# Where the last q/k piece, the first norms and a quarter of the values stand around the attention projection

## Chip, core, metric

The kernel runs on one core of one Trainium2 chip. The metric is device time in microseconds of one execution, the median of several.

## What is computed

One adaLN transformer block on x of shape 2 x 2048 x 256, float32: LayerNorm with modulation, causal attention with random features (16 heads of width 16, 128 features), projection and gated residual, a second LayerNorm, and a feed-forward part with a top-2 router over 4 experts that share Wi and Wo and differ by a rank-4 term.

```python
h = layernorm(x) * (1 + ca) + sa
q, k, v = split(h @ W_attn + b_attn)                  # q, k scaled by 1/sqrt(16)
phi(z) = exp(z @ omega - 0.5 * sum(z * z)) / sqrt(m)  # per head
y = (phi_q . cumsum(phi_k v)) / (phi_q . cumsum(phi_k) + 1e-6)
x = x + ga * (y @ W_proj + b_proj)
h = layernorm(x) * (1 + cb) + sb
w = top2(softmax(h @ Wg.T + bg))
x = x + gb * sum_e w_e * (relu(h @ Wi.T + (h @ A_e.T) @ B_e.T) @ Wo.T)
```

The term sum(z * z) is what the kernel calls norms.

## The kernel before

The 4096 tokens are worked in NB = 8 blocks of T = 512, each four tiles of 128. Every engine runs its own hand-written program; semaphores tie them together, and nothing else decides the order. A loop runs blocks 0 to 6 with `front_next` true, so that block n + 1's front part (LayerNorm 1, q and k, norms, values, the first features) is woven into block n. Block 7 is written out behind the loop without a front part.

q and k come in four pieces j = 0 to 3 of 128 rows by 512 tokens (`qk`, L416). A piece is two halves over the contraction (`ks` [0] and [1]), three matmuls each: products are made from a rounded part and a rest (`split3`, L377: L380 to L382). Piece j lies in PSUM bank `qk_bank[j]`: pa[0], pa[1], ring[2], ring[3]. ScalarE then makes the rounded copy and the square of a piece (`front_qk`, L779: L782, L783) and counts `sq_ready`, and VectorE makes the rest (`split_qk`, L1031) and counts `qk_split`. `norms` (L426) multiplies the squares of two pieces by a matrix that sums over a head; it waits until both are squared. Half 0 (pieces 0 and 1) goes to `norm_bank[0]`, half 1 (pieces 2 and 3) to ring[0]. ScalarE rounds them (L789), VectorE makes their rest (L1040) and counts `norm_split`. `values` (L436) makes the values of the four token tiles into the products banks pb[0] and pb[1], 6 matmuls a tile; VectorE moves them to v_ones (L1046).

The stretch around the change is `after_attend`. On TensorE: the first half of piece 3, norms 0, the transposes of y (`y_transpose`, L606; ScalarE copies them out, L843), the second half of piece 3, the projection into pa (`projection`, L620), norms 1, all values, then `ffn_head`: eight transposes of the normalised tokens (L638) into ring[3] and ring[1], the small matmuls of the router logits and low-rank terms (L643), and the first base matmuls, which read h_r and h_l. VectorE adds the projection to the residual (L1155), takes statistics (L1158, L996 to L999), GpSimd makes the reciprocal deviation (L1333, L1336), VectorE normalises tiles 0 and 1 (L1004) and ScalarE tiles 2 and 3 (L848). After the transposes ScalarE makes h_f (L852) and its rounded copy h_r (L856), VectorE the other half of h_f (L1021) and h_l (L1028). h_r and h_l held block n + 1's first LayerNorm output until then, which q, k and values read.

SyncE (`front_moves`, L329) stores each piece of q and k and each half of the norms to DRAM as they are split, and gathers them as xq, from which the features of block n + 1 are made (L493, L498), the first of them among the experts' matmuls of block n.

Of the kernel before, what the change touches and what calls it, by code (L numbers as in the profile page):

```python
# [43 lines left out]
NT = T // P  # L44
# [54 lines left out]
def wait(eng, signal, n, c):  # L99
    eng.wait_ge(signal.sem, signal.at(n, c))  # L100


def build(nc, x, w_attn, b_attn, w_proj, b_proj, omega, wg, bg, wi, wo, lora_a, lora_b, cond, wmod,
          consts, norm_rows, out, parts_out, norms_out):
    ctx = ExitStack()
    with ctx:
# [102 lines left out]
        prod = ctx.enter_context(nc.psum_tensor("prod", [P, NT, 2, P], F32))  # L209
        pb = [prod[:, 2 * b:2 * b + 2].rearrange("p c k m -> p (c k m)") for b in range(2)]  # L210
        qk_bank = [pa[0], pa[1], ring[2], ring[3]]
        norm_bank = [pa[0], ring[0]]
        z_bank = [ring[3], ring[1], ring[0], ring[2]]
        score_bank = lambda q, a: (pa if q else pb)[a]
        proj_bank = lambda tile: pb[tile % 2] if tile < 2 * TILES else ring[tile % 4]
# [160 lines left out]
        def _(pe):  # L376
# [49 lines left out]
            def norms(n, half):  # L426

                wait(pe, sq_ready, n, 2 * half + 2)
                if half == 0:
                    wait(pe, qk_split, n, 1)  # L430
                for j in (2 * half, 2 * half + 1):
                    mm = pe.matmul(norm_bank[half][j * VA:(j + 1) * VA, :], headsum, qk_sq[:, j, :],
                                   start=True, stop=True)
                mm.then_inc(norm_mm.sem, 1)

            def values(n):  # L436
                for t in range(NT):
                    dst = pb[t // 2][:, t % 2 * C:(t % 2 + 1) * C]
                    tt = slice(t * P, (t + 1) * P)
                    for k in range(KT):  # L440
                        mm = split3(dst, h_r[:, k, tt], h_l[:, k, tt],
                                    wa_r[:, k, 2 * C:3 * C], wa_l[:, k, 2 * C:3 * C], k == 0, k == KT - 1)
                    if t % 2:
                        mm.then_inc(v_ps.sem, 1)
# [164 lines left out]
            def projection(n, front_next):  # L609
                wait(pe, yT_done, n, KT)  # L610
                if front_next:
                    wait(pe, qk_split, n + 1, 2)
                    wait(pe, norm_split, n + 1, 1)
                row = n // BLOCKS_PER_ROW
                for t in range(NT):
                    dst = pa[t // 2][:, t % 2 * C:(t % 2 + 1) * C]
                    for k in range(KT):
                        w = wp_ga[:, row, k, :] if isinstance(n, int) else \
                            wp_ga[:, bass.ds(row, 1), k, :].rearrange("p o c -> p (o c)")
                        mm = pe.matmul(dst, yT[:, k, t * P:(t + 1) * P], w, start=k == 0, stop=k == KT - 1)  # L620
                    if t % 2:
                        mm.then_inc(prj_ps.sem, 1)
# [9 lines left out]

            def ffn_head(n, front_next):

                for t in range(NT):
                    wait(pe, h2n_ready[t // 2], n, t % 2 + 1)
                    for k, dst in enumerate((ring[3], ring[1])):
                        mm = pe.transpose(dst[:, t * P:(t + 1) * P], tok[:, t, k * P:(k + 1) * P], ident)  # L638
                        if t == NT - 1:
                            mm.then_inc(h2_ps.sem, 1)  # L640
                for k in range(KT):
                    wait(pe, h2_full[k], n, 1)
                    mm = pe.matmul(ring[2][:], low_t[:, k, :], h_f[:, k, :], start=k == 0, stop=k == KT - 1)  # L643
                    if k == 0:
                        mm.then_inc(tok_free.sem, 1)
                mm.then_inc(lg_ps.sem, 1)
                base(n, 0, [0])
                wait(pe, lg_done, n, 1)
                base(n, 0, [1])
                rows = slice(LOGIT_ROW, LOGIT_ROW + E)  # L650
                for t in range(NT):
                    mm = pe.transpose(pa[0][:, t * E:(t + 1) * E], lg[rows, t * P:(t + 1) * P], ident[rows, rows])
                mm.then_inc(lt_ps.sem, 1)
                base(n, 1)
                if front_next:
                    wait(pe, norm_split, n + 1, 2)
                base(n, 2)
                wait(pe, low_high, n, 1)
                base(n, 3)
# [81 lines left out]
            def after_attend(n, front_next):  # L741
                if front_next:
                    qk(n + 1, 3, [0])
                    norms(n + 1, 0)
                y_transpose(n)
                if front_next:
                    qk(n + 1, 3, [1])
                projection(n, front_next)
                if front_next:
                    norms(n + 1, 1)  # L750
                    values(n + 1)
                ffn_head(n, front_next)
                masks(n)
                experts(n, front_next)
# [9 lines left out]
        def _(act):  # L764
# [80 lines left out]
            def ffn(n, front_next):  # L845
                wait(act, ln2_pool, n, 2)
                for t in range(2, NT):
                    act.activation(tok[:, t, :], xr[:, t, :], ACT.Identity, bias=shift[:, t:t + 1],  # L848
                                   scale=rstd[:, t:t + 1]).then_inc(h2n_ready[1].sem, 1)
                wait(act, mod2c_set, n, 1)  # L850
                wait(act, h2_ps, n, 1)
                act.activation(h_f[:, 0, :], ring[3][:], ACT.Identity, bias=mod2_cols[:, KT:KT + 1],  # L852
                               scale=mod2_cols[:, 0:1]).then_inc(h2_full[0].sem, 1)
                for k in range(KT):
                    wait(act, h2_full[k], n, 1)
                    act.activation(h_r[:, k, :], h_f[:, k, :], ACT.Copy).then_inc(h2_r.sem, 1)  # L856
                wait(act, lg_ps, n, 1)
                act.activation(lg, ring[2][:], ACT.Copy).then_inc(lg_done.sem, 1)
                act.activation(low.bitcast(F32R), ring[2][0:LROWS, :], ACT.Copy).then_inc(low_high.sem, 1)
                wait(act, rt, n, 10)  # L860
                act.activation(exo[:], ex[:], ACT.Exp).then_inc(rt_exp.sem, 1)
                tile = 0
                for f in range(FT + 3):
                    if f < FT:
                        wait(act, z1_ps, n, f + 1)
                        if f >= 4:
                            wait(act, g_low, n, f - 3)
                        act.activation(g[:, f % 4, :], z_bank[f % 4][:], ACT.Relu).then_inc(r1_done.sem, 1)  # L868
                    if f == 0:
                        wait(act, rho_ps, n, 1)  # L870
                        act.activation(rho, pa[1][:], ACT.Copy).then_inc(rho_done.sem, 1)
                    for _ in range(AHEAD.get(f, 0) if front_next else 0):
                        features(n + 1, tile // TILES, [tile % TILES])
                        tile += 1
                    if 1 <= f <= FT:
                        k = f - 1
                        wait(act, g_sum, n, k + 1)
                        if k == 0 and front_next:
                            for signal in qk_out:
                                wait(act, signal, n + 1, signal.per)  # L880
                        if k >= 3:
                            wait(act, wo_mm, n, k - 2)
                        act.activation(g_r[:, k % 3, :], g[:, k % 4, :], ACT.Copy).then_inc(g_high.sem, 1)  # L883
# [12 lines left out]
            def after_attend(n, front_next):  # L896
                if front_next:
                    front_qk(n + 1, 0)
                    front_qk(n + 1, 1)
                    front_norm(n + 1, 0)  # L900
                y_copy(n)
                if front_next:
                    front_qk(n + 1, 2)
                    front_qk(n + 1, 3)
                    front_norm(n + 1, 1)
                ffn(n, front_next)
# [9 lines left out]
        def _(dve):  # L916
# [364 lines left out]

            def after_attend(n, front_next):
                if front_next:
                    split_norm(n + 1, 0)
                    split_qk(n + 1, 2)
                residual(n)
                if front_next:
                    split_qk(n + 1, 3)
                normalize_apply(n, xr, ln2_pool, h2n_ready[0])
                if front_next:  # L1290
                    split_norm(n + 1, 1)
                h2_copy(n)
                if front_next:
                    values(n + 1, [0])
                split_h(n, h2_r, 1, h2_parts)
                if front_next:
                    values(n + 1, [1])
                ffn_rest(n, front_next)
# [111 lines left out]
```

## Time and profile before

| | us |
|---|---|
| median of 3 runs | 826.2 (823.42, 826.2, 828.61) |
| the profiled execution | 827.64 |
| its span, first to last instruction | 825.9 |
| TensorE busy | 766.3 |
| VectorE busy | 547.2 |
| ScalarE busy | 409.9 |
| mean granted TensorE clock, of full | 0.980 |

Rows of a timeline give start, duration, engine, line, what was written from what, and the idle time of the engine before it with what ended it. Ends of matmuls are modelled and overlap the next one's start, so intervals are best read from start to start. A matmul row in plain float32 counts two instructions per matmul of the program.

### The profile page before, as it was taken

The page shows a single profiled execution, that of the slowest core. Times are in us where ns is not written, and L with a number is a line of the kernel's source. Part 1 is how long each engine was busy: PE and PEld are TensorE (multiplying, and loading weights), DVE is VectorE, ACT ScalarE, POOL GpSimd, SP SyncE. Part 2 cuts the span into 40 slices and gives each one's busy share as a digit, 9 for nine tenths or more (in the row PEclk, how much of TensorE's full clock was granted, in tenths as well). Part 3 has the DMA queues.
Part 4 walks back from the last instruction along what each step waited for, and adds up shares of the span by engine and source line. Part 5 has one row for each costly group of instructions (what it writes and reads, how often), then busy time and mean ns, then how long its engine had stood idle before and what let it go on. Part 6 is the DMA issues. An engine that isn't in the chain of part 4 may idle for free.

```text
span 825.9 us, 16957 instructions
## 1 busy us (share of the span) xinstructions
PE 766.3 (93%) x6138; PEld 605.5 (73%) x6138; DVE 547.2 (66%) x1289; ACT 409.9 (50%) x758; POOL 46.9 (6%) x62
## 2 busy tenths in 40 slices
PE   2989999999999999999999999999999999998696
PEld 2767767977688767977688766977679776886466
DVE  5546666776766766776766766776667767666356
ACT  2365544664366444654466545555446643663222
POOL 1101000010000100010000100010000100010000
PEclk9969999999999999999999999999999999999689
DMA  8680073202802064101722046020732028010000
GB/s 270 145 203 5 2 207 81 77 0 70 213 2 76 0 172 113 51 26 51 191 43 76 0 117 169 0 76 0 206 79 76 0 74 209 2 52 2 0 1 26
DMA packets 46540, 65.37 MB, mean 79 GB/s; under 512 B 8716, under 2 KB 22840, under 8 KB 46392
## 3 DMA queue, kind: packets, MB, share of 16 engines
q1 hardware_dynamic: 46520, 65.10, 29.4%
q8 instruction: 13, 0.21, 0.1%
q14 instruction: 7, 0.06, 0.0%
HBM read 39.87 MB, written 25.17 MB: 79 GB/s over the span
## 4 chain that ended last, share of the span: by engine, by line
PE 85%; DVE 9%; ACT 2%; issue 1%; SPq 1%; DMA 1%; DVEq 0%; POOL 0%; POOLq 0%; ACTq 0%
PE pa L514 11%; PE prod L529 7%; PE ring L493 6%; PE ring L380 6%; PE pa L380 5%; PE ring L381 4%; PE ring L382 4%; PE pa L382 4%; PE pa L381 4%; PE prod L548 4%; PE pa L620 4%; PE ring L498 3%; PE ring L643 2%; PE prod L514 2%; PE ring L696 2%; PE prod L538 2%
## 5 line engine op out<-in xcount | busy, mean ns | idle before, releaser
L514 PE MATMUL pa<-phq,phkT 128*128 128x128 f32 x896 | 115.6, 276 | 0.0
L514 PEld LDWEIGHTS pa<-phq,phkT 128*128 128x128 f32 x896 | 108.4, 192 | 2.4 <-issue 1.6
L821 ACT ACTIVATE phq<-ring 128x512 f32<-128x512 f32 x96 | 58.9, 614 | 91.3 <-PE ring L493 90.3
L1078 DVE TENSOR_TENSOR am_phk<-pa,const 128x512 f32<-128x512 f32 x112 | 74.3, 686 | 33.2 <-PE pa L514 33.2
L1231 DVE SCALAR_TENSOR_TENSOR am_phk<-ring,am_phk 128x512 f32<-128x512 f32 x64 | 44.3, 692 | 53.2 <-PE ring L696 53.2
L380 PE MATMUL pa<-wo_r,qk_r 128*128 128x256 f32 x256 | 72.1, 282 | 0.6 <-DVE qk_l L1236 0.6
L382 PE MATMUL pa<-wo_l,qk_r 128*128 128x256 f32 x256 | 72.2, 282 | 0.0
L883 ACT ACTIVATE qk_r<-phq 128x512 fp32r<-128x512 f32 x64 | 40.5, 632 | 63.7 <-DVE phq L1240 63.7
L381 PE MATMUL pa<-wo_r,qk_l 128*128 128x256 f32 x256 | 71.8, 281 | 0.0
L529 PE MATMUL prod<-am_phk,v_ones 128*32 128x256 f32 x1024 | 61.9, 382 | 4.6 <-DVE tg L1109 4.6
L380 PE MATMUL ring<-h_r,wi_r 128*128 128x512 f32 x128 | 57.9, 452 | 4.2 <-DVE am_phk L1231 3.6
L821 ACT ACTIVATE phkT<-ring 128x512 f32<-128x512 f32 x96 | 59.3, 618 | 0.0
L493 PE MATMUL ring<-xq,omega_x 100*128 100x512 f32 x192 | 58.9, 428 | 0.0
L821 ACT ACTIVATE am_phk<-ring 128x512 f32<-128x512 f32 x96 | 52.9, 614 | 11.3 <-PE ring L498 11.3
L868 ACT ACTIVATE phq<-ring 128x512 f32<-128x512 f32 x64 | 37.6, 587 | 32.8 <-PE ring L684 32.8
L529 PEld LDWEIGHTS prod<-am_phk,v_ones 128*32 128x32 f32 x1024 | 31.3, 109 | 28.9 <-DVE am_phk L1078 6.3
L381 PE MATMUL ring<-h_r,wi_l 128*128 128x512 f32 x128 | 50.9, 398 | 0.0
L382 PE MATMUL ring<-h_l,wi_r 128*128 128x512 f32 x128 | 50.8, 397 | 0.0
L380 PEld LDWEIGHTS pa<-wo_r,qk_r 128*128 128x128 f32 x256 | 48.4, 189 | 2.6 <-DVE qk_l L1236 1.0
L381 PEld LDWEIGHTS pa<-wo_r,qk_l 128*128 128x128 f32 x256 | 48.4, 189 | 1.4
L382 PEld LDWEIGHTS pa<-wo_l,qk_r 128*128 128x128 f32 x256 | 48.1, 188 | 0.0
L1236 DVE TENSOR_TENSOR qk_l<-phq,qk_r 128x512 fp32r<-128x512 f32 x64 | 43.8, 685 | 5.9 <-ACT qk_r L883 5.6
(189 smaller groups left out, 1568.2 us busy)
## 6 DMA issues: line engine op xcount, KB each, us to landing
xq<-qk_parts SPq DMA_DIRECT2D x48, 512.0 KB
qk_parts<-qk_r SPq DMA_DIRECT2D x32, 256.0 KB, 3.6
qk_parts<-qk_l SPq DMA_DIRECT2D x32, 256.0 KB, 4.0
tok<-in_L_attn_x SPq DMA_DIRECT2D x8, 512.0 KB, 4.9
xr<-in_L_attn_x SPq DMA_DIRECT2D x8, 512.0 KB, 4.0
out_x<-tg SPq DMA_DIRECT2D x16, 256.0 KB, 2.2
norm_parts<-norm_r SPq DMA_DIRECT2D x16, 128.0 KB, 3.6
norm_parts<-norm_l SPq DMA_DIRECT2D x16, 128.0 KB, 5.1
```

The costliest lines, as they stand in the source:

```text
L380: pe.matmul(dst, w_r, v_r, start=first, stop=False, skip_group_check=shared)
L381: pe.matmul(dst, w_l, v_r, start=False, stop=False, skip_group_check=shared)
L382: return pe.matmul(dst, w_r, v_l, start=False, stop=last, skip_group_check=shared)
L493: mm = pe.matmul(dst[:], omega_x[:, k // 2 * M:(k // 2 + 1) * M], xq[:, p // HALF, k % 2, p % HALF, :], start=True, stop=True)
L514: mm = pe.matmul(score_bank(q, a)[:, tt], phkT[:, q % 2, a, tt], phq[:, q // 2 % 2, 2 * (q % 2) + a, tt], start=True, stop=True)
L529: mm = pe.matmul(prod[j * VA:(j + 1) * VA, c], v_ones[:, c, GROUP * gr + j, :], both, start=True, stop=True)
L821: act.activation(dst, src, ACT.Exp).then_inc(exp_done.sem, 1)
L868: act.activation(g[:, f % 4, :], z_bank[f % 4][:], ACT.Relu).then_inc(r1_done.sem, 1)
L883: act.activation(g_r[:, k % 3, :], g[:, k % 4, :], ACT.Copy).then_inc(g_high.sem, 1)
L1078: dve.tensor_tensor(am[:, 2 * (q % 2) + a, :].rearrange("p (c t) -> p c t", c=NT), score_bank(q, a)[:].rearrange("p (c t) -> p c t", c=NT) ...
L1231: dve.scalar_tensor_tensor(r2[:, f % 2, :], z_bank[f % 4][:], 0.0, rho, ALU.max, ALU.mult).then_inc(r2_done.sem, 1)
L1236: dve.tensor_tensor(g_l[:, k % 3, :], g[:, k % 4, :], g_r[:, k % 3, :].bitcast(F32), ALU.subtract).then_inc(g_low.sem, 1)
```

## The change

Within `after_attend`, for blocks 0 to 6:

- TensorE: the transposes of y come before norms 0, and the second half of piece 3 comes behind the projection, directly ahead of norms 1. Only three token tiles of the values follow; the fourth is made in `ffn_head` behind the eight token transposes.
- Norms 0 go to pb[0], a products bank, instead of pa[0]. So the projection waits no longer for `norm_split` 1, and `values` does (in the setup too, for block 0). `norms` waits no longer for `qk_split`. `ffn_head` waits for `qk_split` 4 and `norm_split` 1.
- ScalarE does piece 2 ahead of the copy of y and norms 0 behind it, and waits for the last values (`v_ps`) before it writes h_r. VectorE splits piece 2 ahead of norms 0.

```diff
--- before.py
+++ after.py
@@ -209,7 +209,7 @@
         prod = ctx.enter_context(nc.psum_tensor("prod", [P, NT, 2, P], F32))
         pb = [prod[:, 2 * b:2 * b + 2].rearrange("p c k m -> p (c k m)") for b in range(2)]
         qk_bank = [pa[0], pa[1], ring[2], ring[3]]
-        norm_bank = [pa[0], ring[0]]
+        norm_bank = [pb[0], ring[0]]
         z_bank = [ring[3], ring[1], ring[0], ring[2]]
         score_bank = lambda q, a: (pa if q else pb)[a]
         proj_bank = lambda tile: pb[tile % 2] if tile < 2 * TILES else ring[tile % 4]
@@ -426,15 +426,14 @@
             def norms(n, half):
 
                 wait(pe, sq_ready, n, 2 * half + 2)
-                if half == 0:
-                    wait(pe, qk_split, n, 1)
                 for j in (2 * half, 2 * half + 1):
                     mm = pe.matmul(norm_bank[half][j * VA:(j + 1) * VA, :], headsum, qk_sq[:, j, :],
                                    start=True, stop=True)
                 mm.then_inc(norm_mm.sem, 1)
 
-            def values(n):
-                for t in range(NT):
+            def values(n, tiles=range(NT)):
+                wait(pe, norm_split, n, 1)
+                for t in tiles:
                     dst = pb[t // 2][:, t % 2 * C:(t % 2 + 1) * C]
                     tt = slice(t * P, (t + 1) * P)
                     for k in range(KT):
@@ -610,7 +609,6 @@
                 wait(pe, yT_done, n, KT)
                 if front_next:
                     wait(pe, qk_split, n + 1, 2)
-                    wait(pe, norm_split, n + 1, 1)
                 row = n // BLOCKS_PER_ROW
                 for t in range(NT):
                     dst = pa[t // 2][:, t % 2 * C:(t % 2 + 1) * C]
@@ -632,12 +630,17 @@
 
             def ffn_head(n, front_next):
 
+                if front_next:
+                    wait(pe, qk_split, n + 1, 4)
+                    wait(pe, norm_split, n + 1, 1)
                 for t in range(NT):
                     wait(pe, h2n_ready[t // 2], n, t % 2 + 1)
                     for k, dst in enumerate((ring[3], ring[1])):
                         mm = pe.transpose(dst[:, t * P:(t + 1) * P], tok[:, t, k * P:(k + 1) * P], ident)
                         if t == NT - 1:
                             mm.then_inc(h2_ps.sem, 1)
+                if front_next:
+                    values(n + 1, [NT - 1])
                 for k in range(KT):
                     wait(pe, h2_full[k], n, 1)
                     mm = pe.matmul(ring[2][:], low_t[:, k, :], h_f[:, k, :], start=k == 0, stop=k == KT - 1)
@@ -741,14 +744,14 @@
             def after_attend(n, front_next):
                 if front_next:
                     qk(n + 1, 3, [0])
+                y_transpose(n)
+                if front_next:
                     norms(n + 1, 0)
-                y_transpose(n)
+                projection(n, front_next)
                 if front_next:
                     qk(n + 1, 3, [1])
-                projection(n, front_next)
-                if front_next:
                     norms(n + 1, 1)
-                    values(n + 1)
+                    values(n + 1, range(NT - 1))
                 ffn_head(n, front_next)
                 masks(n)
                 experts(n, front_next)
@@ -851,6 +854,8 @@
                 wait(act, h2_ps, n, 1)
                 act.activation(h_f[:, 0, :], ring[3][:], ACT.Identity, bias=mod2_cols[:, KT:KT + 1],
                                scale=mod2_cols[:, 0:1]).then_inc(h2_full[0].sem, 1)
+                if front_next:
+                    wait(act, v_ps, n + 1, 2)
                 for k in range(KT):
                     wait(act, h2_full[k], n, 1)
                     act.activation(h_r[:, k, :], h_f[:, k, :], ACT.Copy).then_inc(h2_r.sem, 1)
@@ -897,10 +902,10 @@
                 if front_next:
                     front_qk(n + 1, 0)
                     front_qk(n + 1, 1)
+                    front_qk(n + 1, 2)
+                y_copy(n)
+                if front_next:
                     front_norm(n + 1, 0)
-                y_copy(n)
-                if front_next:
-                    front_qk(n + 1, 2)
                     front_qk(n + 1, 3)
                     front_norm(n + 1, 1)
                 ffn(n, front_next)
@@ -1281,8 +1286,8 @@
 
             def after_attend(n, front_next):
                 if front_next:
+                    split_qk(n + 1, 2)
                     split_norm(n + 1, 0)
-                    split_qk(n + 1, 2)
                 residual(n)
                 if front_next:
                     split_qk(n + 1, 3)
```

The next pieces show what each engine's program has in a row. Line numbers in those of the changed kernel are its own. First TensorE around the transposes of y, before: ring0 and ring1 take the transposes, ring3 is piece 3's bank, and L432 is `norms`.

```order
L432 MATMUL pa0<-phq,const 32x512 [waits qk_split]
L432 MATMUL pa0<-phq,const 32x512
L100 REGISTER_ALU
L606 MATMUL ring0<-const,tg 128x128 [waits y_step]
L606 MATMUL ring0<-const,tg 128x128 x3
L606 MATMUL ring1<-const,tg 128x128 x4
L380 MATMUL ring3<-h_r,wa_r 128x512
L381 MATMUL ring3<-h_r,wa_l 128x512
L382 MATMUL ring3<-h_l,wa_r 128x512
L620 ISA [waits norm_split,qk_split,yT_done]
L620 MATMUL pa0<-wp_ga,phkT 128x256
```

The same place in the changed kernel, where L605 is the transpose (L100 only prepares a wait), L430 `norms` and L618 the projection:

```order
L605 MATMUL ring0<-const,tg 128x128 [waits y_step]
L605 MATMUL ring0<-const,tg 128x128 x3
L605 MATMUL ring1<-const,tg 128x128 x4
L100 REGISTER_ALU
L430 MATMUL prod<-phq,const 32x512 [waits sq_ready]
L430 MATMUL prod<-phq,const 32x512
L618 ISA [waits qk_split,yT_done]
L618 MATMUL pa0<-wp_ga,phkT 128x256
```

The norms went behind the transposes, and the half piece into ring3 left the place between transposes and projection. Where it went is this piece of the changed TensorE program, behind the projection:

```order
L618 MATMUL pa1<-wp_ga,phkT 128x256 x4
L380 MATMUL ring3<-h_r,wa_r 128x512
L381 MATMUL ring3<-h_r,wa_l 128x512
L382 MATMUL ring3<-h_l,wa_r 128x512
L430 MATMUL ring0<-phq,const 32x512 [waits sq_ready]
L430 MATMUL ring0<-phq,const 32x512
L380 MATMUL prod<-wa_r,h_r 128x256 [waits norm_split]
```

Before, the projection was followed by the norms into ring0 at once; now the last half piece stands between them. ScalarE in the same stretch, before (ring2 and ring3 are pieces 2 and 3):

```order
L789 ACTIVATE norm_r<-pa0 64x512 [waits norm_mm]
L100 ISA
L843 ACTIVATE phkT<-ring0 128x512 [waits yT_ps]
L100 REGISTER_ALU
L843 ACTIVATE phkT<-ring1 128x512 [waits yT_ps]
L100 REGISTER_ALU
L782 ACTIVATE qk_r<-ring2,qk_bias 128x512 [waits qk_ps]
L783 ACTIVATE phq<-ring2,qk_bias 128x512
L100 REGISTER_ALU
L782 ACTIVATE qk_r<-ring3,qk_bias 128x512 [waits qk_ps]
L783 ACTIVATE phq<-ring3,qk_bias 128x512
```

and in the changed kernel:

```order
L785 ACTIVATE qk_r<-ring2,qk_bias 128x512 [waits qk_ps]
L786 ACTIVATE phq<-ring2,qk_bias 128x512
L100 ISA
L846 ACTIVATE phkT<-ring0 128x512 [waits yT_ps]
L100 REGISTER_ALU
L846 ACTIVATE phkT<-ring1 128x512 [waits yT_ps]
L792 ACTIVATE norm_r<-prod 64x512 [waits norm_mm]
L100 REGISTER_ALU
L785 ACTIVATE qk_r<-ring3,qk_bias 128x512 [waits qk_ps]
L786 ACTIVATE phq<-ring3,qk_bias 128x512
```

Piece 2 moved ahead of the copies of y, and the norms behind them.

## Rows read from the trace of the kernel before

**Rows 1.** The page, part 1: busy time and share of the span.

```profile
PE 766.3 (93%) x6138; PEld 605.5 (73%) x6138; DVE 547.2 (66%) x1289; ACT 409.9 (50%) x758; POOL 46.9 (6%) x62
```

**Rows 2.** The chain that ended last: start us, us, what.

```profile
393.62 3.72 PE pa L620 x16
```

**Rows 3.** TensorE's timeline, 476 to 500: start us, us, engine, line, operation.

```profile
476.38 1.93 PE L529 MATMUL prod<-am_phk,v_ones 128*32 128x256 f32 x32 [0.48 <-DVE tg L1109]
...
485.55 1.05 PE L432 MATMUL pa<-phq,const 128*32 128x512 f32 x4
486.54 1.09 PE L606 MATMUL ring<-const,tg 128*128 128x128 f32 x8
487.38 0.48 PE L380 MATMUL ring<-h_r,wa_r 128*128 128x512 f32 x1
...
487.93 0.40 PE L382 MATMUL ring<-h_l,wa_r 128*128 128x512 f32 x1
488.50 3.71 PE L620 MATMUL pa<-wp_ga,phkT 128*128 x16 [0.18 <-ACT phkT L843]
492.15 1.05 PE L432 MATMUL ring<-phq,const 128*32 128x512 f32 x4
493.13 0.39 PE L380 MATMUL prod<-wa_r,h_r 128*128 128x256 f32 x1
...
495.96 0.27 PE L382 MATMUL prod<-wa_l,h_r 128*128 128x256 f32 x1
496.22 1.39 PE L638 MATMUL ring<-const,tok 128*128 128x128 f32 x8
498.43 1.98 PE L643 MATMUL ring<-am_phk,low_t 128*128 128x512 f32 x4 [0.82 <-ACT am_phk L852]
499.85 0.79 PE L380 MATMUL ring<-h_r,wi_r 128*128 128x512 f32 x1
```

**Rows 4.** ScalarE's timeline in the same stretch.

```profile
481.08 0.69 ACT L782 ACTIVATE qk_r<-pa,qk_bias 128x512 fp32r<-128x512 f32 x1 [2.31 <-PE pa L382]
481.67 0.68 ACT L783 ACTIVATE phq<-pa,qk_bias 128x512 f32<-128x512 f32 x1
...
487.23 1.09 ACT L843 ACTIVATE phkT<-ring 128x512 f32<-128x512 f32 x2
...
496.03 1.09 ACT L848 ACTIVATE tok<-xr,shift,rstd 128x256 f32<-128x256 f32 x2 [2.18 <-POOL shift L1336]
497.60 0.78 ACT L852 ACTIVATE am_phk<-ring,mod_cols 128x512 f32<-128x512 f32 x1 [0.48 <-PE ring L638]
```

**Rows 5.** VectorE's timeline in the same stretch.

```profile
475.72 0.42 DVE L1109 TENSOR_TENSOR tg<-prod,rden 128x256 f32<-128x256 f32 x1
...
485.46 0.42 DVE L1109 TENSOR_TENSOR tg<-prod,rden 128x256 f32<-128x256 f32 x1
...
495.75 0.73 DVE L1004 TENSOR_SCALAR tok<-xr,mv,rstd 128x256 f32<-128x256 f32 x2 [0.41 <-POOL rstd L1333]
```

**Rows 6.** Timeline of the setup, TensorE and VectorE.

```profile
30.41 0.39 PE L380 MATMUL prod<-wa_r,h_r 128*128 128x256 f32 x1
...
30.08 0.67 DVE L1040 TENSOR_TENSOR norm_l<-pa,norm_r 64x512 fp32r<-64x512 f32 x1
```

**Rows 7.** Timelines of SyncE's queue and of TensorE's first features.

```profile
490.92 2.38 SPq L353 DMA_DIRECT2D xq<-norm_parts  x4
...
508.88 0.47 PE L493 MATMUL prod<-xq,omega_x 100*128 100x512 f32 x1
```

**Rows 8.** Stretches: PE, PEld, DVE, ACT, POOL busy, then PEclk, DMA, GB/s.

```profile
200.00:760.00 560.00, 541.20 (x4440) 429.85 (x4438) 386.34 (x911) 295.58 (x549) 31.25 (x34) 1.00 0.29 79
764.00:766.00 2.00, 1.60 (x32) 0.88 (x32) 0.87 (x4) 0.00 (x0) 0.00 (x0) 0.75 0.00 0
774.00:776.00 2.00, 2.00 (x8) 1.64 (x7) 0.74 (x2) 0.00 (x0) 0.00 (x0) 0.69 0.00 0
```

**Rows 9.** TensorE's timeline in the last block.

```profile
760.02 1.93 PE L529 MATMUL prod<-am_phk,v_ones 128*32 128x256 f32 x32 [1.18 <-DVE tg L1109]
```

More of the change, by code:

```diff
@@ L743, in after_attend @@
                     qk(n + 1, 3, [0])
-                    norms(n + 1, 0)
                 y_transpose(n)
                 if front_next:
-                    qk(n + 1, 3, [1])
+                    norms(n + 1, 0)
                 projection(n, front_next)
                 if front_next:
+                    qk(n + 1, 3, [1])
                     norms(n + 1, 1)
-                    values(n + 1)
+                    values(n + 1, range(NT - 1))
                 ffn_head(n, front_next)
@@ L899, in after_attend @@
                     front_qk(n + 1, 1)
-                    front_norm(n + 1, 0)
+                    front_qk(n + 1, 2)
                 y_copy(n)
                 if front_next:
-                    front_qk(n + 1, 2)
+                    front_norm(n + 1, 0)
                     front_qk(n + 1, 3)
```

## Prediction

> **What bounds the kernel now.** I read the page's engine table first. TensorE is busy for 93% of the span [rows 1], so what counts is the work in its queue and the gaps in it. The chain of waits gives the rhythm: the projection of one block starts at 393.62, that of the next at 488.50 [rows 2, 3], a period of 94.9 us, and seven of the eight blocks run with the next block's front part woven in. The change touches only the few microseconds around the projection of these seven, and a little of the setup. TensorE's timeline for that stretch [rows 3] shows the order to be followed, those of ScalarE and VectorE [rows 4, 5] what each step waits for. Three gaps are visible. The projection starts after an idle time of 0.18 us. The eight transposes L638 take 1.39 us where those of L606 take 1.09, so they lose 0.30. Before L643 TensorE is idle for 0.82 us. Together 1.3 us per block: that is all the change can win here, 9.1 us over seven blocks.
>
> The two later gaps end a chain that starts with the projection: the residual and its statistics, GpSimd's deviation, tok from VectorE at 495.75 and from ScalarE until 496.03 + 1.09 = 497.12, the last transposes, h_f on ScalarE from 497.60 to 498.38, L643 at 498.43 [rows 3 to 5]. TensorE fills it with the second norms (492.15 to 493.13) and all 24 matmuls of the values.
>
> **The change, step by step,** on the clock of the block in rows 3. I go from start to start, since modelled ends overlap.
>
> *The transposes of y come before the first norms.* They need VectorE's last division, which ends at 485.46 + 0.42 = 485.88. In the same wait one group earlier the division ended at 476.14 and TensorE began at 476.38 [rows 3, 5], so the wake costs 0.24 and the transposes start at 486.12. Before, the norms (L432, 0.99 us) lay there and hid it; now the queue, free at 485.55, stalls for 0.57. This wait is new. From the transposes' start to the next start are 0.84 (486.54 to 487.38), so the norms start at 486.96 and, 0.98 later, the queue reaches the projection at 487.94. Its other condition is ScalarE's copy of y: the transposes end at 487.21, the second copy takes some 0.6 behind that, and the wake was 0.18 (487.23 + 1.09 = 488.32, start at 488.50), so 488.03. ScalarE has done piece 2 before that, since its bank is full before 485.55. The projection starts at 488.03 instead of 488.50: 0.47 won. The first norms cost nothing more in a products bank: the same instructions, and VectorE has read that bank for its last division, on which the transposes ahead of them wait.
>
> *The last half piece follows the projection.* From projection to next start are 3.65, so it starts at 491.68, and its last matmul ends 0.95 later (487.38 to 487.93 + 0.40), at 492.63. The second norms now stand right behind it, and they multiply the squares of this very piece (they wait for sq_ready to reach 4). ScalarE must pass over the bank twice for that: in rows 4 the pair runs from 481.08 to 482.35, 1.27 us, and I let it start 0.04 after the matmul. So the squares are there at 493.94, and with a wake of 0.1 the norms start at 494.05. In the old order the same pair ran beside the projection. The queue alone would have been ready at about 492.5, so this is a new stall of 1.5 us, and everything on TensorE is queued behind it: norms, values, the transposes of the tokens. I see nothing that hides it.
>
> *Three quarters of the values, the transposes, then the last quarter.* Norms to values 0.98 gives 495.03. 18 of 24 matmuls at 0.12 each (493.13 to 495.96 for 23 steps) are 2.1 us: 497.15. The normalised tokens are there by then, since their chain starts 0.47 earlier with the projection: ScalarE's at about 496.65. VectorE's split of the last piece needs the squares at 493.94, and VectorE comes to it only after the statistics, about then, so it delays nothing. The transposes run without a gap from 497.25 to 498.34, and the last quarter of the values (0.7 us) covers ScalarE's h_f, 0.78 plus a wake of 0.05: L643 at 499.15. So the old gap of 0.82 is hidden, all but 0.1 to 0.2. ScalarE's new wait for the last values before it overwrites h_r puts its copy at about 499.2, with h_l on VectorE behind it. Base's first matmul is due 1.42 after L643 (498.43 to 499.85), at 500.57, and h_l comes at about 499.2 + 0.6 + 0.65 + a wake = 500.6. I price this at 0, at most 0.2.
>
> *Sum.* L643 starts at 499.15 instead of 498.43: 0.72 later in each of seven blocks, 5.0 us. What follows (router, masks, experts, the next attention) hangs on L643, so nothing gives it back. Bounds: the wakes seen run from 0.04 to 0.24 and four of them are in the sum, h_l may cost 0.2, and the stall behind the last piece cannot be far under ScalarE's 1.27. That gives 0.3 to 1.1 per block, 2.1 to 7.7.
>
> *Setup.* values(0) now waits for VectorE's first norm split, which ends at 30.08 + 0.67 = 30.75, where it started at 30.41 [rows 6]; with a wake 0.4 us, once. Bounds 0.3 and 0.6.
>
> *Transfers.* The first norm split comes behind ScalarE's copy of y, at about 489.5, some 1.5 us later, and SP's norm stores and the gathers behind them move with it. SP issued the last four of these gathers from 490.92 to 493.30, and their data are first wanted by the features at 508.88, 15 us later [rows 7]. Slack enough: 0.
>
> So the profiled execution, 827.64 us with a span of 825.9, would become 827.6 + 5.0 + 0.4 = 833.0. The median of the three runs shown is 826.2, 1.4 below it; on that scale I forecast 831.6. That is 0.7% slower, and counts as the same: 1%, 8.3 us, is about what a measurement of this kernel can tell from no change.
>
> **The rivals.** *A, slower: TensorE's clock falls.* The change puts stalls of 0.6 and 1.5 us into 8 us, and behind the longer one stand norms on 32 of 128 columns. Over the loop the granted clock is 1.00, which is 2.4 GHz. In the last block, which has no front work in its waits (1.18 us before L529 [rows 9], and shorter ones after it), it fell to 1.2 GHz in the slice 764 to 766 and came back in the slice 774 to 776, ten microseconds later [rows 8]. By these rows a fall costs half of up to 10 us of work; I take 3.5 to 5. In three of seven blocks that is 10.5 or more, 842; in all seven 25 to 35, 857 and up. It outweighs everything else from two blocks on. Against it: the wait of 0.82 between transposes has not done it in any block, and dense matmuls stand on both sides. The Trainium skill, "TensorE: Matmul & The Clock Gate", section "A second HAM failure mode: psum-queue depth-cycling", names frequent short idles between groups of matmuls as a way to lose the clock. By that rule the time would be this rival's; the last block agrees with it, the loop does not show it.
>
> *B, faster: the stall behind the last piece is hidden, and the gaps won count.* If the norms started at once, L643 would be 0.47 earlier with the projection and some 0.7 earlier for the two gaps covered, 1.2 us in all: 826.2 - 8.4 + 0.4 = 818. For it speaks only that the old trace does not show the wait; against it, that ScalarE cannot square a bank before it is written.
>
> *C: it comes out even.* The wakes are all at the low end and the stall before the transposes of y is half of what I take: 0.1 to 0.2 per block, 827 to 828.
>
> **How the numbers follow.** Forecast 0.60 (its own range 828.5 to 834.5), A 0.22, B 0.05, C 0.13. The line of slower by over 1% is 834.5: 0.03 of the forecast lies above it, and 0.19 of A (with one fall it stays below), which makes 0.22. Faster needs 818 or less: 0.03, out of B. The rest, 0.75, is the same. The range runs from 826, under C, to 841, just short of A in three blocks, and leaves out most of A.
>
> **What would show it.** In the changed profile: TensorE's wait of the second norms for ScalarE's square, idle 1.3 or more, seven times; a wait of the transposes of y for VectorE's tg of 0.3 to 0.6; the wait for h_f down from 0.82 to under 0.3; the token transposes in 1.1 us; a period of 95.6; a granted clock of 1.00 between 200 and 760. Wrong would be a period at or under 94.9, a clock below 1.00 in the loop, or a wait for gathers before the features.

## The result, and the profile after

The changed kernel took 830.23 us (median of 13 runs, 828.86 to 831.49) against 826.26 (13 runs): ratio 1.0056, 95% interval 1.0044 to 1.0068. It is slower by half a percent, inside the range, and under the 831.6 forecast. The prediction took 1%, 8.3 us, as about what a measurement can tell from no change; this interval, 0.24% wide, tells much less than that. The profiled execution took 830.51 us with a span of 828.7; before, 827.64 with 825.9.

TensorE is less busy in a longer span, on page part 1 [rows 1]:

```profile
PE 762.5 (92%) x6138; PEld 606.8 (73%) x6138; DVE 546.6 (66%) x1289; ACT 411.2 (50%) x758; POOL 47.1 (6%) x62
```

The chain of waits has the projections of two blocks 95.25 us apart, where they were 94.88 by rows 2 and 3. This distance is called the period below:

```profile
394.22 3.65 PE pa L618 x16
...
489.47 3.65 PE pa L618 x16
```

TensorE's timeline of the same block as in rows 3. L605 is the transposes of y, L430 the norms, L618 the projection, L639 the token transposes, L646 what was L643:

```profile
486.14 0.48 PE L380 MATMUL ring<-h_r,wa_r 128*128 128x512 f32 x1
...
486.69 0.40 PE L382 MATMUL ring<-h_l,wa_r 128*128 128x512 f32 x1
487.40 1.09 PE L605 MATMUL ring<-const,tg 128*128 128x128 f32 x8 [0.30 <-DVE tg L1114]
488.42 1.05 PE L430 MATMUL prod<-phq,const 128*32 128x512 f32 x4
489.40 3.72 PE L618 MATMUL pa<-wp_ga,phkT 128*128 x16
492.77 0.58 PE L380 MATMUL ring<-h_r,wa_r 128*128 128x512 f32 x1
...
493.42 0.40 PE L382 MATMUL ring<-h_l,wa_r 128*128 128x512 f32 x1
495.17 1.05 PE L430 MATMUL ring<-phq,const 128*32 128x512 f32 x4 [1.36 <-ACT phq L786]
496.15 0.39 PE L380 MATMUL prod<-wa_r,h_r 128*128 128x256 f32 x1
...
498.38 1.04 PE L639 MATMUL ring<-const,tok 128*128 128x128 f32 x8
499.18 0.36 PE L380 MATMUL prod<-wa_r,h_r 128*128 128x256 f32 x1
...
500.24 1.98 PE L646 MATMUL ring<-am_phk,low_t 128*128 128x512 f32 x4
501.69 0.76 PE L380 MATMUL ring<-h_r,wi_r 128*128 128x512 f32 x1
```

ScalarE in the same stretch [rows 4]: the copies of y (L846), the pair on piece 3 (L785, L786), the tokens, h_f (L855).

```profile
488.09 1.09 ACT L846 ACTIVATE phkT<-ring 128x512 f32<-128x512 f32 x2 [0.97 <-PE ring L605]
...
493.85 0.69 ACT L785 ACTIVATE qk_r<-ring,qk_bias 128x512 fp32r<-128x512 f32 x1 [3.74 <-PE ring L382]
494.44 0.68 ACT L786 ACTIVATE phq<-ring,qk_bias 128x512 f32<-128x512 f32 x1
...
496.93 1.10 ACT L851 ACTIVATE tok<-xr,shift,rstd 128x256 f32<-128x256 f32 x2
499.41 0.78 ACT L855 ACTIVATE am_phk<-ring,mod_cols 128x512 f32<-128x512 f32 x1 [1.38 <-PE ring L639]
```

VectorE: the last division and the tokens [rows 5].

```profile
486.92 0.42 DVE L1114 TENSOR_TENSOR tg<-prod,rden 128x256 f32<-128x256 f32 x1
...
496.65 0.74 DVE L1009 TENSOR_SCALAR tok<-xr,mv,rstd 128x256 f32<-128x256 f32 x2 [0.41 <-POOL rstd L1338]
```

Both new waits are there. The transposes of y stand idle for 0.30 us behind VectorE's division. The second norms stand idle for 1.36 us: piece 3's last matmul starts at 493.42, ScalarE's two passes run from 493.85 to 495.12, and the norms start at 495.17. The gap before L646 is gone, and the token transposes take 1.04 us instead of 1.39. TensorE's waits over the run say the same (who waited, for whom, us, times, longest). Of the eight for L786 one is in the setup, of the eight for L1114 the longest is in the last block, and so is the only one for L855:

```profile
PE ring L430 <- ACT phq L786: 9.9, 8, 1.4
...
PE ring L605 <- DVE tg L1114: 3.2, 8, 1.0
...
PE ring L646 <- ACT am_phk L855: 0.7, 1, 0.7
```

In the setup the values start at 30.80, 0.39 later than in rows 6:

```profile
30.80 0.39 PE L380 MATMUL prod<-wa_r,h_r 128*128 128x256 f32 x1 [0.32 <-DVE norm_l L1045]
```

SyncE's last four gathers went out 2.86 us later than in rows 7. Of that 1.46 is because this trace is later as a whole (the first half of piece 3 starts at 486.14, against 484.68), so 1.4 is the change's, forecast 1.5. The features started unhindered:

```profile
493.78 2.38 SPq L353 DMA_DIRECT2D xq<-norm_parts  x4
```

```profile
510.67 0.47 PE L492 MATMUL prod<-xq,omega_x 100*128 100x512 f32 x1
```

TensorE's clock stayed at 2.4 GHz (PEclk 1.00, third figure from the end) throughout the loop [rows 8]:

```profile
200.00:760.00 560.00, 537.78 (x4433) 430.00 (x4433) 384.46 (x907) 297.13 (x549) 31.31 (x34) 1.00 0.30 79
```

### The profile page after: what moved, and what is told of

Read it like the earlier page. It is cut to its first block, busy times and chain, and to the rows that moved or that the text cites. A ratio compares the mean times of both kernels' runs of the same rounds, so it can differ in the third digit from the quotient of the medians.

```text
span 828.7 us, 16963 instructions
## 1 busy us (share of the span) xinstructions
PE 762.5 (92%) x6138; PEld 606.8 (73%) x6138; DVE 546.6 (66%) x1289; ACT 411.2 (50%) x758; POOL 47.1 (6%) x62
## 4 chain that ended last, share of the span: by engine, by line
PE 82%; DVE 10%; ACT 4%; issue 2%; SPq 1%; DMA 1%; DVEq 0%; POOL 0%; ACTq 0%
PE pa L513 11%; PE prod L528 7%; PE ring L492 6%; PE ring L380 5%; PE pa L380 5%; PE pa L382 4%; PE pa L381 4%; PE ring L381 4%; PE ring L382 4%; PE prod L547 4%; PE pa L618 4%; PE ring L497 3%; PE ring L646 2%; PE prod L513 2%; PE prod L537 2%; PE prod L554 2%
## 5 line engine op out<-in xcount | busy, mean ns | idle before, releaser
L528 PE MATMUL prod<-am_phk,v_ones 128*32 128x256 f32 x1024 | 61.9, 382 | 4.6 <-DVE tg L1114 4.6
```

Of the source, the lines that this page charges most:

```text
L528: mm = pe.matmul(prod[j * VA:(j + 1) * VA, c], v_ones[:, c, GROUP * gr + j, :], both, start=True, stop=True)
```

## The experiments

Each was timed beside the kernel before, on the same chip. The theory: in the kernel before, LayerNorm 2's chain sets when L643 can start, and TensorE's work in between only fills it; in the changed kernel TensorE waits in every block for squares that it needs, and is late for the end of that chain.

### The second norms behind the values

```diff
 after_attend on TensorE
-                    norms(n + 1, 1)
                     values(n + 1, range(NT - 1))
+                    norms(n + 1, 1)
 ffn on ScalarE, behind its two token tiles
+                if front_next:
+                    front_norm(n + 1, 1)
```

> The changed kernel with one more move: on TensorE the second norms stand behind the three tiles of values instead of ahead of them, and ScalarE rounds them behind its two token tiles. Theory (the wait of the second norms for ScalarE's squares, 1.36 us idle in each of seven blocks of the changed trace, is the loss): the values hide ScalarE's pair, the wait goes, and the stretch is bound by LayerNorm 2's chain, which takes 9.93 us from the projection's start to L643 in the old trace. The projection starts 3.26 us after the first half of piece 3 in the changed trace, so L643 comes at 13.19 instead of 14.10 (changed) or 13.75 (before): period 94.3 to 94.5, ratio to before 0.995 (0.993 to 0.997). Rival (the loss lies in the stall before the transposes of y or in the products bank): the ratio stays at 1.004 or more. Rival (the last quarter of the values behind the token transposes delays the chain): 0.998 to 1.001.

Measured: ratio to before 0.9972 (0.9953 to 0.9992), median 824.63 of 12 runs. The period was 94.52. TensorE's timeline:

```profile
484.90 1.09 PE L605 MATMUL ring<-const,tg 128*128 128x128 f32 x8 [0.31 <-DVE tg L1115]
...
486.90 3.72 PE L618 MATMUL pa<-wp_ga,phkT 128*128 x16
...
493.37 1.05 PE L430 MATMUL ring<-phq,const 128*32 128x512 f32 x4
494.62 1.39 PE L639 MATMUL ring<-const,tok 128*128 128x128 f32 x8 [0.20 <-DVE tok L1010]
...
497.00 1.98 PE L646 MATMUL ring<-am_phk,low_t 128*128 128x512 f32 x4 [0.28 <-ACT am_phk L857]
```

The wait for the squares is gone, and only order was changed: that wait was the loss. Of its 1.36 us only 0.73 of a period came back (95.25 to 94.52), because then LayerNorm 2's chain sets the end again. The projection starts 2.00 behind the transposes of y, as in the changed kernel. L646 comes 10.10 behind it, not 9.93. ScalarE shows why: its norms (L792) now stand ahead of h_f (L857) and hold it up.

```profile
495.55 0.59 ACT L792 ACTIVATE norm_r<-ring 64x512 fp32r<-64x512 f32 x1
496.17 0.78 ACT L857 ACTIVATE am_phk<-ring,mod_cols 128x512 f32<-128x512 f32 x1
```

### The last quarter of the values alone

```diff
 kernel before, ffn_head
+                if front_next:
+                    values(n + 1, [NT - 1])
 after_attend on TensorE
-                    values(n + 1)
+                    values(n + 1, range(NT - 1))
 ffn on ScalarE, ahead of h_r
+                if front_next:
+                    wait(act, v_ps, n + 1, 2)
```

> The kernel before with one part of the change alone: the last tile of the values is made behind the token transposes, with ScalarE's new wait. Theory (L643 hangs on the chain from the projection over VectorE, GpSimd and ScalarE, and TensorE's work only fills it): the values fill the gap of 0.82 us but the tokens are not ready earlier, so L643 starts when it did; ratio 1.000 (0.999 to 1.001), the gap appears ahead of the transposes instead. Rival (the gap is TensorE's to win): 0.7 us in seven blocks, ratio 0.994.

Measured: 0.9996 (0.9978 to 1.0014). The gap moved:

```profile
487.69 3.72 PE L620 MATMUL pa<-wp_ga,phkT 128*128 x16 [0.18 <-ACT phkT L845]
...
495.40 1.40 PE L638 MATMUL ring<-const,tok 128*128 128x128 f32 x8 [0.69 <-DVE tok L1008]
...
497.62 1.55 PE L645 MATMUL ring<-am_phk,low_t 128*128 128x512 f32 x3
```

L645 is the old L643. The gap before it is closed, and one of 0.69 us has opened before the token transposes. From the projection to L645 are 9.93 us, as before. Filling a gap in a chain wins nothing when the chain sets the end.

### The half piece back ahead of the projection

```diff
 changed kernel, after_attend on TensorE
-                projection(n, front_next)
                 if front_next:
                     qk(n + 1, 3, [1])
+                projection(n, front_next)
+                if front_next:
```

> The changed kernel with one part undone: the second half of piece 3 stands ahead of the projection again, behind the first norms. Theory: the wait for the squares goes (ScalarE's pair lies beside the projection), the projection starts 0.70 later than in the changed kernel, at 3.96 after the first half piece, and the chain puts L643 9.93 behind it, 13.89 against 13.75 before: period 95.1, ratio 1.001 (1.000 to 1.002), and clearly under the changed kernel's 1.0056. Rival (the stall before the transposes of y and the swap of norms and transposes make the loss): ratio 1.004 or more.

Measured: 1.0012 (0.9992 to 1.0032), with projections at 394.51 and 489.55, a period of 95.04. The interval leaves out the changed kernel's 1.0056. In the loop 0.21 us of a block came back (95.25 to 95.04), as the theory has it; that makes 1.5 of the 3.6 us between the two ratios. The remainder is not in the loop; "Where the 4.0 us are" below takes it up. TensorE's timeline has no wait for the squares left. From the first half of piece 3 (485.33) to L646 (499.22) are 13.89 us, as expected, against 13.75 before. The wait for the transposes of y is still there:

```profile
486.59 1.09 PE L605 MATMUL ring<-const,tg 128*128 128x128 f32 x8 [0.31 <-DVE tg L1115]
```

### The pair run twice, and one pass more

```diff
 changed kernel, ScalarE, ahead of front_qk(n + 1, 3)
+                    wait(act, qk_ps, n + 1, 4)
+                    act.activation(phkT[:, 1, 0, :], qk_bank[3][:], ACT.Identity, bias=qk_bias[:, 3:4])
+                    act.activation(phkT[:, 1, 1, :], qk_bank[3][:], ACT.Square, bias=qk_bias[:, 3:4])
```

The second of these two kernels has the Square alone.

> The changed kernel with ScalarE's pair on piece 3 run twice, the first time into a buffer nobody reads, so that the wait of the second norms is 1.15 to 1.27 us longer in each of seven blocks. Theory (all of that wait is on the path): 8.0 to 8.9 us over the changed kernel, ratio to before about 1.0155, the wait's idle time 2.5 us, granted clock 1.00 in the loop. Rival (a longer wait makes TensorE's clock fall): a granted clock under 1.00 in the stretch behind the norms and 3.5 us or more for each fall, ratio 1.02 and up. Rival (part of the wait is covered by the chain): under 4 us over the changed kernel.

> The changed kernel with one pass of ScalarE more (a Square of piece 3 into a buffer nobody reads) ahead of the pair for which the second norms wait. Theory (the wait is on the path in full, and the clock falls only when it grows further): about 0.57 us more in each of seven blocks, period 95.8, 4 us over the changed kernel, ratio to before 1.0105, granted clock 1.00 in the loop. Rival (the fall that the doubled pair brought in four of seven blocks sets in here already): some periods of 97.4, 1.55 us longer than the others, ratio 1.013 or more.

Measured with the pair: 1.0214 (1.0186 to 1.0243), median 842.49 of 6, some 13 us over the changed kernel. The chain shows two kinds of block, 97.93 and 96.45 us long:

```profile
206.70 3.65 PE pa L618 x16
...
304.63 3.65 PE pa L618 x16
...
401.08 3.65 PE pa L618 x16
```

The short ones are 1.2 over the changed kernel's 95.25, which is ScalarE's added pair; the wait grew from 1.36 to 2.51. In the long ones the clock fell. These stretches stand right behind the wait of a long block and at the same place of a short one; PEclk is the third figure from the end:

```profile
115.00:117.00 2.00, 1.40 (x4) 0.19 (x4) 1.40 (x3) 0.55 (x1) 1.08 (x2) 0.64 1.06 197
117.00:119.00 2.00, 2.00 (x9) 1.54 (x8) 0.69 (x1) 1.40 (x3) 0.00 (x0) 0.51 1.06 213
...
311.00:313.00 2.00, 1.50 (x8) 0.66 (x9) 1.40 (x3) 0.85 (x2) 0.98 (x2) 1.00 1.05 197
313.00:315.00 2.00, 2.00 (x19) 2.00 (x19) 0.69 (x1) 1.29 (x3) 0.00 (x0) 1.00 1.07 214
```

That happened in four of the seven blocks and cost 1.5 us each: from the projection to L646 are 13.5 us in those and 12.0 in the others. Why some of these blocks lost the clock and others, with the same wait, did not, no run shows.

With one pass more the ratio was 1.0094 (1.0065 to 1.0124), median 832.78 of 6: 8.3 us over its own runs of before, where the changed kernel was 4.0 over, so 4.3 for the pass. In its profiled execution, the longest of the six at 836.89, four of the six periods are 95.8 us and two 97.3: two blocks of seven lost the clock, at 1.5 us each again. Its wait:

```profile
PE ring L430 <- ACT phq L786: 13.9, 8, 1.9
```

So the wait is on the path in full. From the projection to L646 are 10.85 us in the changed kernel, and in blocks that kept the clock 11.42 and 12.01: 0.57 for a wait longer by 0.57, and 1.16 for 1.15. And the clock was lost behind a wait of 1.9 us in two blocks and of 2.5 us in four.

### No quarter

The kernel of the first experiment with all four value tiles ahead of the norms.

```diff
-                    values(n + 1, range(NT - 1))
+                    values(n + 1)
                     norms(n + 1, 1)
 ffn_head
-                if front_next:
-                    values(n + 1, [NT - 1])
```

> The version with the second norms behind the values, but with all four tiles of the values ahead of the norms and none behind the token transposes. Theory (the quarter only fills a gap of the chain): the transposes wait 0.7 us less, L643 comes where it did or up to 0.3 us later; period 94.5 to 94.8, ratio to the kernel before within 0.002 of that version's 0.997. Rival (the quarter behind the transposes is what wins): 0.7 us in seven blocks more, ratio 1.003.

Measured: 0.9983 (0.9961 to 1.0004), a period of 94.50. The quarter does nothing here either: 94.50 and 94.52 are the same period, and the two intervals overlap.

### The half piece as filler

```diff
-        norm_bank = [pb[0], ring[0]]
+        norm_bank = [ring[0], ring[0]]
 after_attend on TensorE
                 y_transpose(n)
                 if front_next:
-                    norms(n + 1, 0)
+                    qk(n + 1, 3, [1])
                 projection(n, front_next)
                 if front_next:
-                    qk(n + 1, 3, [1])
-                    norms(n + 1, 1)
+                    norms(n + 1, 0)
                     values(n + 1, range(NT - 1))
+                    norms(n + 1, 1)
```

ScalarE squares piece 3 ahead of norms 0, and VectorE splits norms 0 only behind the residual and piece 3. The norms 1 of ScalarE and VectorE stand behind h_r and h_l, and `values` does not wait for `norm_split`.

> A version meant to be the fastest: transposes of y first as in the change, the second half of piece 3 (0.7 us) as the filler between them and the projection, both norms behind the projection in ring[0] (half 0 at once, half 1 behind three tiles of values), ScalarE's and VectorE's work on norms 1 behind h_f and h_l. Theory (the stretch is bound by the chain division, transposes of y, copy, projection, LayerNorm 2, h_f, L643): the projection starts up to 0.16 us earlier than in the version with the norms behind the values, and h_f is no longer held up by ScalarE's norms (0.16): period 94.2 against 94.52 there and 94.93 before, ratio to before about 0.994 (0.992 to 0.997). Rival: the norms' stores and the gathers behind them now leave some 4.5 us later than before, the first features (9.7 us behind L643) wait for them, and the time is at 1.000 or over, with a wait of the features for a DMA in the trace.

Measured: 1.0518 (1.0486 to 1.0549), 866.67 us. The stretch itself did what was expected, 9.92 to 9.93 us from the projection to the old L643 (108.41 to 118.33, 208.44 to 218.37). The rival came true, but at another place than I had named: not the features waited but VectorE's first mask product, which overwrites norm_r and so needs the norms' stores to have landed.

```profile
DVE norm_r L1228 <- DMA norm_parts<-norm_l: 37.2, 7, 5.6
```

SyncE's stores and gathers of one block, and the product:

```profile
518.00 0.50 SPq L342 DMA_DIRECT2D norm_parts<-norm_r  x1
...
520.94 2.38 SPq L353 DMA_DIRECT2D xq<-norm_parts  x4
...
525.94 0.60 SPq L342 DMA_DIRECT2D norm_parts<-norm_l  x1
```

```profile
534.06 0.68 DVE L1228 TENSOR_TENSOR norm_r<-am_phk,pa 96x512 fp32r<-96x512 f32 x1 [5.42 <-DMA norm_parts<-norm_l]
```

The first norm store left at 518.00, 7.45 us behind this block's projection (510.55; in the changed kernel it is 1.45); the gathers and the stores of pieces 2 and 3 followed, and the last norm store, out at 525.94, landed only after VectorE had waited 5.42 us. TensorE, idle meanwhile for 5.18 us, then lost its clock in each of the seven blocks (granted 0.50 from 532 to 538 in this one), which adds to the 42 us.

### The rounding of the norms behind h_f

The kernel of the first experiment, with `front_norm(n + 1, 1)` on ScalarE moved behind h_r and `split_norm(n + 1, 1)` on VectorE behind `split_h`.

```diff
 ffn on ScalarE
-                if front_next:
-                    front_norm(n + 1, 1)
                 wait(act, mod2c_set, n, 1)
...
                     act.activation(h_r[:, k, :], h_f[:, k, :], ACT.Copy).then_inc(h2_r.sem, 1)
+                if front_next:
+                    front_norm(n + 1, 1)
 after_attend on VectorE
-                if front_next:
-                    split_norm(n + 1, 1)
                 h2_copy(n)
...
                 if front_next:
+                    split_norm(n + 1, 1)
                     values(n + 1, [1])
```

> The version with the second norms behind the values, with ScalarE's rounding and VectorE's split of these norms moved behind h_f, h_r and h_l. Theory (L643 hangs on h_f, which ScalarE's norms held up by 0.16 us; nothing else waits for the second norms before base's third tile, and their stores, some 3 us later, land before the masks need the buffer, which in the kernel with the half piece as filler they did not): from the projection's start to L643 9.93 instead of 10.09, period 94.36, ratio to before 0.996 (0.994 to 0.998). Rival (3 us is too much for the stores): VectorE's first mask product waits for a DMA and the period is over 94.6.

Measured: 0.9965 (0.9943 to 0.9987), median 823.19 of 12. The period is 94.33, by the chain:

```profile
391.87 3.67 PE pa L618 x16
...
486.20 3.66 PE pa L618 x16
```

From the projection to L646 are 9.93 us in all seven blocks, and no mask product waited for a transfer. This version is faster than the kernel before and than the changed one. Its projection comes as early as the changed kernel's, and the chain behind it takes no longer than before: that is the part of the change that wins.

## Why the prediction was right, and what was mis-sized

*The stall behind the half piece* was the step that decided, and it was right: forecast 1.5 us, measured idle 1.36, and 1.35 from that matmul's end (493.82) to the norms. Taking it away by order alone turned the loss into a gain (0.9972), undoing the half piece's move alone gave back 0.21 of a period and brought the ratio to even (1.0012), and lengthening it lengthened the block one for one, besides the lost clock.

*The size* was too high: 0.72 per block forecast, 0.35 measured. From the first half of piece 3 to L643 the old block took 13.75 us (484.68 to 498.43), the new one 14.10 (486.14 to 500.24), and the forecast was 14.47.

```profile
484.68 0.48 PE L380 MATMUL ring<-h_r,wa_r 128*128 128x512 f32 x1
```

Two terms carry that. The wake, the time from the last condition to the start, was taken as 0.24 for the transposes of y, from L529, which waits for more than the division; it was 0.06 (487.34 to 487.40). Half of this was lost again: from the transposes' start to the projection's are 2.00 us, where the sum had 1.91, so the projection came after 3.26 us and not 3.35. And the half piece behind the projection was taken from a place in another company: projection to its last matmul's end was 3.65 + 0.95 = 4.60 in the sum and 493.82 - 489.40 = 4.42 in the trace. The rest, 0.1, is the wake of the norms, 0.05 where 0.1 stood, and the token transposes, 1.04 where 1.09 stood. The term for h_l, priced at 0, was 0.03: base's first matmul came 1.45 behind L646 (500.24 to 501.69), where it had come 1.42 behind L643.

*The transposes of y*: a stall of 0.57 forecast, some 0.4 measured by starts (0.71 from the last matmul of the half piece to the transposes; before, 0.32 from the same matmul to the norms), and it was more than paid for: the projection came 0.56 earlier in the block, forecast 0.47.

*The gap of 0.82*: hidden, as forecast. But the quarter of the values is not what the kernel needed; alone it is worth nothing (0.9996), and without it the better order is as fast to within the interval (0.9983). Here the prediction's opening was wrong: it counted the two gaps at the end of LayerNorm 2's chain among the 1.3 us per block that could be won. From the projection to L643 no version took less than 9.8 us; the best one won 0.6 of a period (94.9 to 94.33), and 0.56 of that is the earlier projection.

*The setup*: 0.4 forecast, 0.39 measured. *The transfers*: no wait, as forecast. I had named the features as the first reader of these transfers; the tighter one is VectorE's mask product, which the half-piece version met.

*Where the 4.0 us are.* In the profiled executions the first L643 came 0.38 later than before (119.18 against 118.80) and the seventh 2.48 later (690.77 against 688.29): 0.35 per block. The first figure holds the setup's 0.4 and that block's own 0.35, less some 0.35 for which no step of the change accounts: the block began at 56.06 instead of 55.66 while the clock, still at half, came up at 61.5 instead of 61.9, so 0.7 us less of it ran at half clock. At their ends the two profiled executions differ by 2.87. The medians differ by 3.97. The other 1.1 us goes, as far as the runs show, with the mean granted clock. Of the 29 executions of the kernel before beside the first four experiments, the 13 at 0.980 took 826.97 to 828.02 us, the 10 at 0.987 or 0.988 took 822.30 to 824.21; the changed kernel's 13 all lie between 0.978 and 0.984, and its profiled execution, at 0.978, is near its median, where the one of before, at 0.980, is 1.4 above its own. So 830.2 came as near to 831.6 partly by luck. From one profiled execution to the other the sum of 5.4 us was 2.9, 830.5 instead of 833.0; the prediction's step from there to the median, 1.4 less, did not hold for the changed kernel (0.3 less), and that gave 1.1 back. The profiles show a difference of this kind in the last block, which has no front work: here the kernel before (0.980) and the third experiment (0.985) from 760 to their ends, PEclk third from the end.

```profile
760.00:826.00 66.00, 49.38 (x284) 36.70 (x284) 33.88 (x85) 15.66 (x28) 1.38 (x2) 0.85 0.03 9
```

```profile
760.00:823.00 63.00, 45.37 (x284) 34.19 (x284) 34.82 (x89) 15.55 (x28) 1.38 (x2) 0.92 0.03 9
```

Why the changed kernel should lose more clock there more often was not tried; its last block is the same code, started at another time. That stays open.

*The rivals.* A did not happen in the changed kernel: no block of the loop below 1.00. But it stood near: 0.55 us more of wait brought the fall in two blocks of seven, 1.15 in four. Its price was mis-sized: 1.5 us a fall, not 3.5 to 5, because in the loop the clock was back after some 4 us, where the last block had it down for ten. By that price all seven would have given 10.5 us, not 25. The Trainium skill ("TensorE: Matmul & The Clock Gate", "A second HAM failure mode: psum-queue depth-cycling") names frequent short idles between groups of matmuls as a way to lose the clock. These two kernels agree in part: idles of 1.9 and 2.5 us cost the clock, but what was varied was the length of one idle per block, and no run here shows what their frequency does. B was excluded by the wait itself, and its price of 1.2 us per block was too high as well: with the wait gone the first experiment won 0.4. C (even) was excluded by the interval. But the wakes were at the low end and the stall before the transposes of y was 0.4 of 0.57, as C had it, and the profiled executions alone differ by 2.9 us, between C and the forecast.

## What to carry to other kernels

When an instruction stream is reordered, look first at what directly follows a moved piece: here a consumer of its result, with another engine's two passes between them. A gap at the end of a chain is not a place to put work; ask what the chain starts with and bring that forward. And count for every store not only who reads its data, but who overwrites its source.

## What was not expected of the hardware

- TensorE lost its clock behind waits of 1.9 us (two of seven blocks) and 2.5 us (four of seven), followed by norms on 32 columns, though dense matmuls stood on both sides, and not behind 1.36 us (none of seven). Each fall cost 1.5 us.
- The time from another engine's last instruction to TensorE's start was 0.05 to 0.06 us for the norms behind ScalarE (495.12 to 495.17), the transposes behind VectorE (487.34 to 487.40) and L646 behind h_f (500.19 to 500.24). The 0.24 seen at L529 is not a general price, and neither is this: the projection of the kernel before, which waits for three counts, started 0.18 behind ScalarE's copy (488.32 to 488.50).
- Executions of one kernel, the one before, differed by 4 to 5 us of 825 with their mean granted clock, 0.980 against 0.987 or 0.988.
